# The set-up of a six-stage decoder kernel merged into its first attention, with a new order of that stage's parts

## What is computed

```python
def _L0_attn_ref(x, Wq_d, bq_d, W_qk, b_qk, Wkv_d, bkv_d, Wv_u, bv_u, Wo, bo):
    C_q = x @ Wq_d + bq_d                      # 512 -> 12
    C_kv = x @ Wkv_d + bkv_d                   # 512 -> 4, shared by the 32 heads
    q = (C_q @ W_qk + b_qk).reshape(b, s, 32, 4)
    scores = jnp.einsum('bqhd,bkd->bhqk', q, C_kv) / jnp.sqrt(4)
    attn = jax.nn.softmax(scores, axis=-1)
    V = (C_kv @ Wv_u + bv_u).reshape(b, s, 32, 16)
    out = jnp.einsum('bhqk,bkhd->bqhd', attn, V).reshape(b, s, 512)
    return out @ Wo + bo
x = x + _L0_attn_ref(_layernorm(x), ...)
```

## Time and profile before

| what | us |
|---|---|
| median of three runs | 1384.99 |
| the profiled execution | 1389.86 |
| its span | 1388.2 |
| set-up and its end, to the first normalisation | 38.03 |
| first normalisation to first exponential | 23.02 |
| 31 intervals between the exponentials of the 32 units | 166.45 |

### The profile page before, as it was taken

How to read it: one execution, slowest core, us unless ns; L and a number is a source line. 1 busy time by engine, 2 the same in 40 slices (tenths; PEclk the granted TensorE clock), 3 DMA queues, 4 the chain that set the end, 5 groups by cost and what they waited for, 6 DMA issues and landing times. The chain is left out here.

```text
span 1388.2 us, 24433 instructions
## 1 busy us (share of the span) xinstructions
PE 1176.0 (85%) x9406; PEld 620.0 (45%) x9406; DVE 761.2 (55%) x1332; ACT 413.2 (30%) x649; POOL 404.8 (29%) x324
## 2 busy tenths in 40 slices
PE   3797988398898797998899999999587769999993
PEld 1354544166666443444344444444354434444441
DVE  6465554268888686635721521521389932556466
ACT  2364553155554112521111211211133313222220
POOL 2265433688882000007800000000122310134152
PEclk9677755589999898999899999999799969999997
DMA  5000000111110101422100000000000000000000
GB/s 171 17 10 10 1 1 1 35 40 41 41 37 3 38 0 33 150 74 86 52 0 1 0 0 0 0 1 0 9 12 9 4 23 1 1 30 15 15 31 30
DMA packets 28042, 35.53 MB, mean 26 GB/s; under 512 B 4602, under 2 KB 19219, under 8 KB 27956
## 3 DMA queue, kind: packets, MB, share of 16 engines
q1 hardware_dynamic: 26888, 32.97, 7.5%
q10 hardware_dynamic: 1068, 1.34, 0.3%
HBM read 30.10 MB, written 4.19 MB: 25 GB/s over the span
## 5 line engine op out<-in xcount | busy, mean ns | idle before, releaser
L1582 DVE TENSOR_TENSOR d_h_low<-d_hf,d_h_high 128x512 f16<-128x512 f32 (+1 forms) x40 | 32.2, 805 | 205.9 <-ACT d_h_high L1639 205.9
L109 PE MATMUL d_p_up<-d_xt_high,wd_hi 128*128 128x512 f16 (+1 forms) x352 | 134.0, 381 | 2.9 <-PE d_p_y L111 1.5
L110 PE MATMUL d_p_up<-d_xt_low,wd_hi 128*128 128x512 f16 (+1 forms) x352 | 133.9, 380 | 0.0
L111 PE MATMUL d_p_up<-d_xt_high,wd_lo 128*128 128x512 f16 (+1 forms) x352 | 133.9, 380 | 0.0
L109 PE MATMUL d_p_y<-wd_hi,d_h_high 128*128 128x512 f16 (+1 forms) x272 | 104.8, 385 | 3.1 <-DVE d_h_low L1582 3.1
L110 PE MATMUL d_p_y<-wd_lo,d_h_high 128*128 128x512 f16 (+1 forms) x272 | 104.7, 385 | 0.0
L111 PE MATMUL d_p_y<-wd_hi,d_h_low 128*128 128x512 f16 (+1 forms) x272 | 104.7, 385 | 0.0
L552 POOL TENSOR_TENSOR a_pt_low<-a_ex,a_pt_high 128x1024 f16<-128x1024 f32 x32 | 68.5, 2142 | 110.4 <-ACT a_pt_high L784 110.4
L1778 POOL MEMSET e_wskip<- 128x128 f32 x1 | 0.2, 204 | 300.1 <-POOLq L1508 300.1
L386 ACT ACTIVATE d_sg<-d_p_up 128x512 f32<-128x512 f32 (+1 forms) x40 | 23.7, 593 | 211.9 <-PE d_p_up L111 211.9
L631 DVE TENSOR_REDUCE a_top<-a_p_s 128x16 f32<-128x1024 f32 x32 | 39.2, 1225 | 64.2 <-PE a_p_s L889 64.1
(11 more groups left out here) (310 smaller groups left out, 3018.4 us busy)
## 6 DMA issues: line engine op xcount, KB each, us to landing
wd_raw<-in_w_d SPq DMA_DIRECT2D x16, 616.0 KB, 3.8
wd_raw<-in_w_f SPq DMA_DIRECT2D x8, 578.0 KB, 3.7
X<-in_x SPq DMA_DIRECT2D x4, 1024.0 KB, 12.7
b_kt<-in_ctx_t SPq DMA_DIRECT2D x128, 32.0 KB
out_x<-wd_raw SPq DMA_DIRECT2D x16, 256.0 KB, 2.0
b_cd<-in_ctx SPq DMA_DIRECT2D x32, 64.0 KB, 2.3
wd_raw<-in_w_c SPq DMA_DIRECT2D x4, 274.0 KB, 2.6
wo<-in_Wo ACTq DMA_DIRECT2D x1, 1024.0 KB
```

The source lines that it names most:

```text
L109: nc.tensor.matmul(ps, st[0], mv[0], start=start, stop=False)
L110: nc.tensor.matmul(ps, st[0], mv[1], start=False, stop=False)
L111: return nc.tensor.matmul(ps, st[1], mv[0], start=False, stop=stop)
L1582: nc.vector.tensor_tensor(hid[1][0:n, d % NH, :], value, hid[0][0:n, d % NH, :], ALU.subtract).then_inc(h_ready, 1)
```

## The change

`setup_stage` is gone, and its work stands in `stage_a`. The scratch tensors lie in `wd_hi` and `wd_lo`, which a later stage fills (so the order shows them under these names). SyncE loads two chunks of X first, then the fold's weights, the other two chunks and the rest; the small loads that the query weights need are issued by ScalarE. Statistics are computed by chunk: chunk 0 at once, chunk 1 after the first normalisations, chunks 2 and 3 after peaks in chunk 0, and GpSimd computes the inverse deviations of each chunk by itself. The two products of the fold are front parts W of units 4 and 6; masks and the rest of the preparation are made after the peaks of units 1, 4 and 5. The zero rows of `bd` and of `wqk` are written once, on VectorE; the eight rows of ones for the shift are written by ScalarE in two halves.

For chunks 1 to 3 the keys are spread by SyncE: 24 copies per chunk, of four rows each, from `keys` into `bd`; chunk 0 still uses VectorE's masked copies. The maxima are kept in bf16, and turned by bf16 products (the margin TOP under which the exponential is kept is lowered with it). A query product takes all 121 rows of keys, of which 96 meet zero weights, where it took 25. The ring has one query and one output per unit. VectorE does a part of a unit's tasks before its peak (`before_peak`), the rest after it (`after_peak`); the statistics of an updated tile follow apart (`measure`). The weights of the third stage are split by ScalarE and VectorE in the last chunk, no longer by GpSimd.

```diff
--- before.py
+++ after.py
...
-TOP = 10 * math.log(2.0)
+TOP = 2 * math.log(2.0)
...
-def setup_stage(nc, held, a):
...
+        top = sb("top", [128, 2, UH], BF16)
...
+        spare = held.wd_hi[:].bitcast(F32)
+        wo = spare[:, 0:4 * D].rearrange("p (o n) -> p o n", o=4)
...
-        ring = {0: [("T", 0), ("T", 1)], 1: [("T", 2), ("Z", 0)], 2: [("T", 3), ("O", 0)], 3: [("L", 0), ("O", 1)],
-                4: [("O", 2), ("V", 0)], 5: [("Q", 0), ("Q", 1)], 6: [("Q", 2), ("Q", 3)], 7: [("O", 3)]}
-        first = [("T", 0), ("T", 1), ("T", 2), ("T", 3), ("L", 0), ("V", 0), ("Q", 0), ("Q", 1), ("Q", 2), ("Q", 3)]
+        ring = {0: [("T", 1, 2), ("T", 1, 3)], 1: [("L", 1, 0)], 2: [("V", 1, 0), ("Z", -1, 0)],
+                3: [("Q", 1, 0), ("O", -1, 0)], 4: [("Q", 1, 1), ("O", -1, 1)], 5: [("Q", 1, 2), ("O", -1, 2)],
+                6: [("Q", 1, 3), ("O", -1, 3)], 7: [("T", 2, 0), ("T", 2, 1)]}
+        fold = {4: ("W", 0, 0), 6: ("W", 0, 1)}
+        first = [("T", 0, 0), ("T", 0, 1), ("T", 0, 2), ("T", 0, 3), ("L", 0, 0), ("V", 0, 0),
+                 ("Q", 0, 0), ("Q", 0, 1), ("Q", 0, 2), ("Q", 0, 3)]
+        second = [("T", 1, 0), ("T", 1, 1)]
...
+                def spread(c):
+                    sp.wait_ge(keys_ready, c + 1)
+                    sp.wait_ge(bd_clear, 2)
+                    if c >= 2:
+                        sp.wait_ge(st_ready, 2 * TC * (c - 1))
+                    for h in range(8):
+                        for r in range(3):
+                            p = slice(32 * r + DL * h, 32 * r + DL * h + DL)
+                            fetch(bd[p, c % 2, :, h, :], keys[p, :].rearrange("p (b k) -> p b k", k=S), bd_in)
...
+                fetch_x(0)
+                fetch_x(1)
+                fetch(wv_t, a["Wv_uT"].rearrange("(o p) d -> p o d", p=128), par_b)
+                fetch(wo, a["Wo"].rearrange("(o p) n -> p o n", p=128), par_b)
+                fetch(bv_col, a["bv_uT"], par_b)
+                fetch(bo, row(a["bo"]), par_b)
+                fetch_x(2)
+                fetch_x(3)
...
+                for c in range(1, NC):
+                    spread(c)
+                for q in range(2, NP_C):
+                    fetch_weights(q)
...
+                def rstd(c):
+                    tiles = slice(TC * c, TC * c + TC)
+                    pool.wait_ge(x_stats, 2 * TC * (c + 1))
+                    nc.gpsimd.tensor_scalar(held.ve[:, tiles], held.mv[:, tiles, 1], EPS, None,
+                                            ALU.add).then_inc(held.rs_ready, 1)
+                    pool.wait_ge(held.rs_ready, 2 * c + 1)
+                    nc.gpsimd.tensor_tensor(held.rstd[:, tiles, 0], held.ve[:, tiles], held.mhalf[:, tiles],
...
-                def split_step(m):
...
+                    if n in (4, 8):
+                        rstd(2 + n // 8)
...
+                def stats_x(c):
+
+                    v.wait_ge(x_in[c], 16)
+                    for i in range(TC):
+                        nc.vector.bn_stats(xst[:, i, :], held.X[:, TC * c + i, :]).then_inc(x_stats, 1)
+                    v.wait_ge(x_stats, 2 * TC * c + TC)
+                    for i in range(TC):
+                        nc.vector.bn_aggr(held.mv[:, TC * c + i, :], xst[:, i, :]).then_inc(x_stats, 1)
+                    v.wait_ge(x_stats, 2 * TC * c + 2 * TC)
...
-                def tasks(c, j):
...
+                def before_peak(c, j):
+                    if j == 0 and more:
+                        norm(c + 1, 2)
                         norm(c + 1, 3)
-                    if j == 2 and tail:
-                        low_z(c - 1)
-                    if j == 3 and tail:
-                        update(c - 1, 0)
-                    if j == 4:
-                        if more:
-                            make_keys(c + 1)
-                        if tail:
-                            update(c - 1, 1)
-                    if j == 5:
+                    if j == 2 and more:
+                        make_keys(c + 1)
+                    if j == 3:
                         if more:
                             values(c + 1)
-                            spread(c + 1, range(0, 4))
                         if tail:
-                            update(c - 1, 2)
-                    if j == 6 and more:
-                        low_query(c + 1, 0)
-                        low_query(c + 1, 1)
-                        spread(c + 1, range(4, 8))
-                    if j == 7 and more:
-                        low_query(c + 1, 2)
-                        low_query(c + 1, 3)
-                        if c + 2 < NC:
-                            norm(c + 2, 0)
-                            norm(c + 2, 1)
+                            low_z(c - 1)
+                    if j >= 4:
+                        if more:
+                            low_query(c + 1, j - 4)
+                        if tail:
+                            update(c - 1, j - 4)
+                    if c == 0 and j == 5:
+                        split_wvo()
+                    if c == 0 and j == 7:
+                        split_bvo()
+
+                def after_peak(c, j):
+
+                    if c == 0:
+                        if j == 0:
+                            stats_x(2)
+                        if j == 1:
+                            spread_values()
+                        if j == 3:
+                            stats_x(3)
+                        if j == 4:
+                            make_masks()
+                        if j == 5:
+                            make_rest()
+                    elif j >= 4:
+                        measure(c - 1, j - 4)
+                    if j == 6 and c + 2 < NC:
+                        norm(c + 2, 0)
+                        norm(c + 2, 1)
+                    if c == NC - 1 and 0 <= j < NP_C:
+                        low_weights(j)
+                nc.vector.memset(kq_raw, 0.0).then_inc(kq_clear, 1)
+                nc.vector.memset(held.wkq[:, :, 96 + 2 * QL:97 + 2 * QL], 0.0).then_inc(wkq_ready, 1)
...
+                stats_x(0)
+                query_weights()
                 for i in range(TC):
                     norm(0, i)
+                stats_x(1)
                 make_keys(0)
-                spread(0, range(8))
+                spread_first(range(8))
                 values(0)
                 for g in range(4):
...
+                    if n < N:
+                        before_peak(n // 8, n % 8)
                     if n + 1 < N:
                         peak(n + 1)
                     if n >= 3 and n % 2:
                         norm_z((n - 3) // 2)
                     if n < N:
-                        tasks(n // 8, n % 8)
-                update(NC - 2, 3)
+                        after_peak(n // 8, n % 8)
...
+                for use in first:
                     front(use)
+                    if use[0] == "L":
+                        delta(1)
                 shift(0)
+                for use in second:
+                    front(use)
                 for n in range(N):
...
-                                                w[96:KQ, g, :, :].rearrange("p a n -> p (a n)"), keys[96:KQ, :],
+                                                w[0:KQ, g, :, :].rearrange("p a n -> p (a n)"), keys[0:KQ, :],
...
+                def fold_weights(i):
+                    pe.wait_ge(wv_ready, 8)
+                    both = wv_bd if i == 0 else bv_rep
+                    for o in range(4):
+                        left = both[:, o, :, :].rearrange("p h d -> p (h d)") if i == 0 else both[:, o, :]
+                        last = nc.tensor.matmul(bank(("W", 0, i)), left, wo[:, o, :], start=o == 0, stop=i == 0 and o == 3)
+                    if i:
+                        last = nc.tensor.matmul(bank(("W", 0, i)), held.ones[0:1, :], bo, start=False, stop=True)
+                    last.then_inc(fold_ready, 1)
+
...
-                                                held.ident[:], start=True, stop=True)
+                                                held.ident16[:], start=True, stop=True)
...
-                setup_stage(nc, held, a)
```

498 lines of the change are left out of this document (240 added, 258 removed).

## The result

The changed kernel takes **1343.39 us** (median of 4 runs, 1340.29 to 1349.59); the kernel before, run beside it, 1386.43 us (1381.89 to 1388.52). The ratio is **0.9699**, with a 95% interval of 0.9656 to 0.9743: faster by 3.0%. The forecast was 1353 us. The profiled execution took 1349.59 us (span 1347.8) against 1389.86 (span 1388.2), 40.3 us less.

What follows compares the result with a forecast made beforehand. TensorE was taken to set the loop's period wherever it has front work, ScalarE elsewhere, VectorE the set-up's end. Terms -24.2 + 6.4 - 12.4 - 1.8 = -32.0 us gave 1357.9 profiled, 1353 us median; own range 1342 to 1364, eight in ten 1328 to 1374.

Steps and rivals of the forecast that it cites:

- The start: Up to the first exponential: X loaded first brings it from 61.05 to 36.8 us, -24.2 us, bounds -20.2 and -25.7.
- the low-clock rival: TensorE's clock stays low: latents at the start 3.4 us dearer, chunk 0 +15, median 1372 us; chance 0.15.
- Chunk 0: First chunk takes in set-up work, chiefly the weight fold: 43.4 against 37.03 us, +6.4 us.
- The folds: Weight-fold products in two units of chunk 0: 6.56 and 8.2 us low, 3.3 and 4.1 high; summed as 5.5 and 5.0.
- The statistics behind the peaks: Two rounds in chunk 0, 2.9 us each on VectorE, beside front work: cost 0; uncovered, one would cost 1.5.
- Chunks 1 and 2: The two full chunks, with new order and cheaper peaks: 84.6 against 96.97 us, -12.4 us; all low -5.0, all high -30.6.
- the clock stays high through the queries: Rival: query units keep the high clock, using all rows and never waiting for a bank; median 1318 us, chance 0.17.
- The peaks at the low clock: TensorE's peak products in each unit: two bf16 products take 0.20 us where four f32 records took 0.95.
- Chunk 3: Last chunk, which has only outputs: 30.6 against 32.45 us, -1.8 us (high clock -9.6).
- The split of the third stage's weights: Moved into chunk 3's gaps on ScalarE and VectorE: cost 0; uncovered, about half a microsecond for each of four.
- The keys by DMA: 24 copies per chunk on SyncE take 15.5 us, with 27 us before the scores read them, so nobody waits.

Runs made afterwards that it cites:

- e11: Changed kernel with the four loads of X issued behind the twelve other loads of SyncE's queue; ratio 0.9752, first exponential at 46.58 us.
- e1: Changed kernel with its query products back on 25 rows instead of 121; 1351.18 us, ratio 0.9762, chunks 1 and 2 took 76.46 us.
- e4: Changed kernel with the peaks kept in 32 bits and turned by 32-bit products; 1345.40 us, ratio 0.9709.
- e12: Changed kernel with the late splits of e5, plus 32-bit peaks in chunk 3 alone; 1337.45 us, ratio 0.9679, chunk 3 took 26.85 us.
- e7: Kernel before with its query products over 121 rows, nothing else of the change; 1390.26 us, ratio 1.0013.
- e9: Kernel before with 16-bit peaks and the offset that goes with them, nothing else of the change; 1373.00 us, ratio 0.9913.
- e6: Changed kernel with one of the four products of each fold, three left out; 1345.32 us, ratio 0.9717, chunk 0 took 40.03 us.
- e5: Changed kernel with VectorE's splits of folded output weights and bias moved behind peaks, W_c's low parts one unit after ScalarE's high parts; 1335.98 us, ratio 0.9645.
- e3: Changed kernel with the kernel before's order of units and VectorE spreading the keys; 1371.35 us, ratio 0.9887, chunks 1 and 2 took 88.17 us.
- e2: Changed kernel with the keys of chunks 1 to 3 spread by VectorE, no copies by DMA; 1355.67 us, ratio 0.9787.

## Why the prediction was right, and which term was not

**The start** was right in its steps and 2.45 us short. X landed and the first normalisation came as worked out, and e11 shows that the start follows X's place in the queue. Most of the difference is the clock under the first latents: 6.16 us in the profiled execution of the changed kernel, 3.67 in those of e1, e4 and e12, whose program is the same up to there and whose first exponential came at 37.4 to 37.7. The kernel before varies alike: 3.67 us in its own profile, 6.18 in e7's and 5.72 in e9's, with starts of 61.05, 63.69 and 62.64. So part of the measured -21.75 is which execution was profiled: 2.5 of the 3.4 us that the low-clock rival held. The last 0.6 to 0.9 us are open.

**Chunk 0** was right in size (+7.15 for +6.4) and half wrong in cause; that the sizes agree is luck. The folds came out nearly as priced: 5.1 and 6.2 us on TensorE, 11.4 together, for the 10.5 in the sum; dropping three quarters of their products gave back 4.15 us (e6). VectorE's splits of the folded weights, which I had at nothing, cost up to 5.0 (e5): they stood ahead of a peak that TensorE waited for, 1.95 us at 66.5 and 1.70 at 81.5. The other units were cheaper than priced by about as much, at a clock of 0.88 where the kernel before had 0.73. The statistics behind the peaks cost nothing that shows: their two units took 3.5 and 3.2 us (priced 4.3 and 3.7).

**Chunks 1 and 2** is the mis-sized term: -24.0 for -12.4. The mechanism, no bank waits and cheaper peaks, was right. Going from one kernel to the other, the peaks gave 9.6 (e9), the rows and the rest of the set-up's move lost 0.8 (e9 to e3), the order gave 7.0 (e3 to e2) and the copies 8.2 (e2 to after); each step is one profile against another and may be off by some 3 us. What failed is the step that priced query units at the low clock, 5.5 us each, because "the clock was low through the queries after them": they ran at the full clock, 3.3 to 4.5 us from peaks to peaks, 15.8 for the four where 22.0 stood in the sum, as the rival "the clock stays high through the queries" had it for these chunks. Twice 6.2 us is the whole miss of 11.6 and a little more. The median of 1343.39 still lies in the forecast's own range (1342 to 1364), at its lower end; the start, 2.45 short, hid a part of the miss. The peaks at the low clock were priced too cheap, 0.20 us for the measured 0.30, which is small beside it. My argument against that rival, that the values' tiny products bring the clock down, is refuted: they are still there, at 132.2, and the clock stayed at 1.00 from 128 to 155.

Ahead of most falls stands a wait of TensorE: 0.92 us, ended at 119.18 in the kernel before (the clock fell at 120.8), 2.23 us at 103.05 in e2 (103.8), in the changed kernel 1.95 us at 66.5 (66.6), 1.70 us at 81.5 (83.8) and 1.63 us at 116.16 (117.9). In e1 it fell at 104.8 with no wait above 0.4 us but with queries on 25 rows, and in chunk 0 of the changed kernel it fell near 56.3 behind waits of no more than 0.73 us. The kernel before's long wait of 5.27 us came behind the fall, so it is not its cause. That waits cause the falls is argued from these places and doesn't cover them all; no run changed a wait alone, so why the clock stays up in the query units remains open.

The parts don't add up by themselves. Alone in the kernel before, peaks gave 0.9%, copies nothing (0.9945 to 1.0010), rows nothing. Undone alone in the changed kernel, peaks cost nothing and copies 0.9%. It is in the new order that the copies are nearly free.

**The rival "the clock stays low"** fell. The rule on transposes (the Trainium skill, "TensorE: Matmul & The Clock Gate", Part 4) says that transposes don't count as busy, and by it the pairs would not raise the clock. The trace leans against it at the start, where sixteen transposes are TensorE's only work in the first 16.2 us of e4:

```profile
L103 PE MATMUL a_p_f<-ident,a_xn x16: 272/421/448, 12.7 to 15.9; 128*128 128x128 f32 x16
```

Their time (ns, minimum, median, maximum) fell from 421 to as little as 272, and the latents behind them ran at the full clock at once, as in e1, e3 and e12; in the changed kernel's own profile all sixteen took 421 or more. So the clock rose under transposes alone (the granted clock on record is 1.00 there throughout, so it is their pace that shows it). The section says it of TensorE's transpose mode, and no row shows whether these f32 products ran in it. The fall at 117.9 us, inside the first transposes of a pair, would fit the rule, but these stood behind a wait of 1.63 us.

**Chunk 3** gave 0.6 us, not 1.8. The last units with an output took 4.7 us, as worked out (4.61). The split of the third stage's weights, put at nothing with an uncovered bound of 2 us, cost 1.9 (e5). With the clock it may have cost more: with 16-bit peaks and no split in this chunk e9 took 25.61 us at a clock of 0.77, with the split e3 took 34.41 at 0.55. No run moved the split alone out of the chunk.

**The keys by DMA** went as forecast but with less room. A copy was issued in 0.637 us, not 0.55, so 24 take 15.3; chunk 3's keys were made near 133 and landed at 150.9, while the faster units left 18 us rather than 27. The wait was 0.6 us once. The 48 us by the fixed cost of the Trainium skill ("DMA: Bandwidth & Descriptors", Anatomy of one DMA), taken in turn, did not show: it was 18 us for 24 copies. The section gives its 2.0 us for copies issued by GpSimd, and these were SyncE's.

## What to carry to other kernels

Look first at what stands on a helper engine ahead of the operation that releases the bounding one, however small: splits of 1.4 and 1.8 us ahead of two peaks made TensorE wait 1.95 and 1.70 us and were worth up to 5.0 us of the chunk, as much as three quarters of the folds (4.15 us). Edits that each gain nothing may only work together (an early producer and a slow transfer), so undo them one at a time in the final version as well as trying them alone. Price a stretch at both clocks: here that choice alone put chunks 1 and 2 off by 11.6 us.

## What the runs showed of the hardware

- The same instructions ran at different clocks in different executions: the first latents took 6.16 or 3.67 us, and chunks 1 and 2 of one code 72.95 or 69.54 us. Such a stage can be told apart from another to some 3 us only; chunk 3, at the low clock nearly throughout, scattered less (31.87 to 32.80 us in five runs).
- Sixteen transposes, TensorE's only work up to then, took 421 ns each by the median and as little as 272 in e4: the clock rose under them.
- Short copies inside the chip's own memory (4 KB, 4 rows) cost SyncE 0.637 us each to issue, 0.1 more than loads of 32 KB from HBM at 0.549.
- The same TensorE products of 121 and of 25 rows took the same time at the same clock (0.63 low); whether the clock stays may depend on the rows, by e1's 3.5 us, which is hardly more than the scatter.
- Peak products of 32 and of 16 bits have no one-way effect on the clock. In the changed kernel 32 bits (4 records, 0.60 us at the full clock) went with 0.94 against 0.88 in chunks 1 and 2 and with 0.80 and 0.72 against 0.50 in chunk 3, but with 0.81 against 0.88 in chunk 0 (e4), and cost nothing measurable on the whole. In the kernel before they went with 0.55 against 0.77 in chunk 3, and 16 bits were 0.9% faster.
